# A four-network graph kernel: zeroing of the table issued behind the first loads, bit planes stored by the scalar engine with four buffers

## The reference

```python
def _L0(node_features, edge_attr, W_msg_tp, W_msg_lin, W_upd_tp, W_upd_lin, edge_index):
    row, col = edge_index
    x_j = node_features[col]
    m = einsum('ei,ej,ijh->eh', x_j, edge_attr, W_msg_tp) / sqrt(128)
    m = silu(m) @ W_msg_lin / sqrt(16)
    agg = segment_sum(m, row, num_segments=6250)
    u = silu(einsum('ni,nh,ihk->nk', node_features, agg, W_upd_tp) / sqrt(256)) @ W_upd_lin / sqrt(16)
    return node_features + u
```

## Time and profile before

| | us |
|---|---|
| median of 3 runs | 11527.22 |
| lowest, highest | 11523.59, 11538.84 |
| the profiled execution | 11525.68 |
| its span | 11523.9 |
| start, until the first matmul of the edge stage | 441.5 |
| first edge stage and N0, until the convolutions' first loads | 441.5 to 2931.4 |
| everything behind | 2931.4 to 11523.9 |

### The profile page before, as it was taken

The page is one execution under the profiler, slowest core; times in us unless marked ns, Lnnn a source line. Parts: engine busy times, 40 slices in busy tenths (PEclk is TensorE's granted clock), DMA queues, the critical chain, the costliest instruction groups (busy, mean ns, idle before and its releaser), DMA issues.

```text
span 11523.9 us, 201355 instructions
## 1 busy us (share of the span) xinstructions
PE 8973.8 (78%) x51270; PEld 6020.0 (52%) x51270; DVE 7298.7 (63%) x14361; ACT 4035.9 (35%) x11725; POOL 6700.9 (58%) x6789
## 2 busy tenths in 40 slices
PE   0499999998488998857666666688888868888886
PEld 0266666663367777742222222455555645555554
DVE  1498999995122222227777777677777767777776
ACT  2445333332000010005555555344444434444443
POOL 0588788777100000007777777577777757777775
PEclk9999999996588888855555555555555555555555
DMA  6733443440887877882222222111111111111111
GB/s 240 249 98 101 119 109 108 108 109 5 290 282 250 269 245 247 296 279 37 39 38 38 38 38 38 25 20 20 20 20 20 20 21 20 20 20 20 20 20 20
DMA packets 1340632, 1146.59 MB, mean 99 GB/s; under 512 B 329039, under 2 KB 1225504, under 8 KB 1340190
## 3 DMA queue, kind: packets, MB, share of 16 engines
q1 hardware_dynamic: 1108690, 1064.47, 29.1%
q0 software_dynamic: 210560, 44.35, 5.2%
q10 hardware_dynamic: 21186, 34.95, 1.2%
HBM read 994.01 MB, written 144.62 MB: 99 GB/s over the span
## 4 chain that ended last, share of the span: by engine, by line
POOL 31%; PE 14%; issue 12%; DMA 8%; DVE 7%; DVEq 1%; ACT 1%; SPq 1%; POOLq 0%; ACTq 0%
POOL arena L569 31%; PE ps L820 8%; DMA arena<-adj 5%; DVE msg L1779 3%; PE ps L754 2%; DVE arena L1774 2%; DMA arena<-tab,idx 2%; PE ps L935 2%; DVE acc L1266 1%; PE ps L797 1%; PE ps L633 1%; ACT x_all L1106 0%; SPq L455 0%; DMA arena<-rT 0%; DVE x_all L1606 0%
## 5 line engine op out<-in xcount | busy, mean ns | idle before, releaser
L569 POOL DMA_INDIRECT arena<-tab,idx x4896 | 4675.6, 955 | 3843.8 <-DMA idx<-in_src_p 2290.4
L935 PE MATMUL ps<-w_w2b,arena 33*128 33x256 f32 x6528 | 2928.1, 639 | 603.1 <-DMA arena<-rT 594.9
L935 PEld LDWEIGHTS ps<-w_w2b,arena 33*128 33x128 f32 x6528 | 2103.8, 330 | 1223.1 <-issue 686.9
L598 POOL DMA_INDIRECT adj<-pairs x1632 | 1868.7, 1145 | 491.4 <-issue 420.8
L1266 DVE TENSOR_TENSOR acc<-acc,ps 48x128 f32 x4920 | 1377.7, 280 | 660.0 <-DVE acc L1266 12.6
L820 PE MATMUL ps<-arena 128*128 128x192 bf16 (+1 forms) x18816 | 1341.5, 234 | 229.9 <-DMA arena<-adj 214.4
L820 PEld LDWEIGHTS ps<-arena 128*128 128x128 bf16 x18816 | 1282.7, 103 | 303.0 <-issue 293.7
L1774 DVE TENSOR_TENSOR arena<-ps,arena 128x512 f32<-128x512 f32 x1632 | 1012.8, 682 | 190.2 <-DMA arena<-tab,idx 186.6
L633 PEld LDWEIGHTS ps<-arena,threes 128*48 128x48 bf16 x4912 | 486.9, 152 | 1232.9 <-issue 1232.9
L633 PE MATMUL ps<-arena,threes 128*48 128x128 bf16 x4912 | 628.1, 309 | 642.5 <-DVE threes L1275 638.1
L1013 ACT ACTIVATE wide<-ps,not_all 128x128 bf16<-128x128 f32 x1632 | 572.8, 377 | 1241.3 <-PE ps L701 1241.1
(11 more groups left out here) (250 smaller groups left out, 10654.0 us busy)
## 6 DMA issues: line engine op xcount, KB each, us to landing
arena<-adj SPq DMA_DIRECT2D x672, 896.0 KB, 7.3
arena<-rels SPq DMA_DIRECT2D x204, 512.0 KB
arena<-tab SPq DMA_DIRECT2D x1632, 64.0 KB
adj<-zero SPq DMA_DIRECT2D x49, 2048.0 KB, 20.8
arena<-tab,idx POOLq DMA_INDIRECT x4896, 2.4
arena<-rT SPq DMA_DIRECT2D x408, 128.0 KB
adj<-pairs POOLq DMA_INDIRECT x1632
rT<-spare ACTq DMA_DIRECT2D x204, 128.0 KB
```

The lines of the kernel that those rows point to most:

```text
L569: pool.indirect_dma_start(G[b][:, u, 0:FEAT[PHASES[p]]], None, TABLE[PHASES[p]], bass.IndirectOffsetOnAxis(ap=idx[b // 2][:, b % 2 * HT + ...
L598: pool.indirect_dma_start(adj_cells, bass.IndirectOffsetOnAxis(ap=pairs[h][:, u, 0:1], axis=0), pairs16[h][:, u, 2:3], None).then_inc(cell ...
L935: last = mm(ps[:, 4 + q, (u % 2) * 256:(u % 2 + 1) * 256], row[h][0:33, u * P:(u + 1) * P], w["w2b"][:, :], start=True, stop=True)
```

## The change

SP issues 41 of the 49 zero DMAs directly behind its loads, and the last 8 (`ZEROS_LATE`) between the loads of batch 2 and batch 3 of the first edge stage. ACT now issues the stores of `rels` and the bit planes; the planes have four buffers. The columns that the 52 sums need are computed by DVE ahead of the bit planes, and ACT does the sums between its other work: ten in the bit planes, two for each chunk of A0, sixteen at the end. A0 has two buffers for its rows and two PSUM banks, is written out chunk by chunk, and PE reads the nodes directly where DVE had copied them. The helpers of the old loop, already unused, go.

```diff
+        bit16 = [x[0:T // TR, o:o + HE].bitcast(bf16) for x, o in ((arena, 2 * HE), (arena, 3 * HE), (spare, 0), (wide_flat, 0))]
+        A_ROWS = [tst[:, :, :].rearrange("p j f -> p (j f)"), stage[:, 0:CH]]
...
+        ZEROS_LATE = 8
...
-            sp.wait_ge(ready, KEYS)
-            sp.dma_start(rels, arena[0:T // TR, 4 * HE:6 * HE]).then_inc(rels_out, 16)
-            for j in range(BITS):
-                sp.wait_ge(bit_cast, j + 1)
-                sp.dma_start(bits[j, :].rearrange("(t e) -> t e", e=TR * P), bit16[j % 2]).then_inc(bits_out[j % 2], 16)
...
-            zero_table()
+            zero_table(0, NS - ZEROS_LATE)
             sp.wait_ge(w_in, 16 * LOADED)
-            sp.wait_ge(tbl_out, tables(1))
+            for j in range(2):
+                sp.wait_ge(rows_stored[j], 16 * ((NC + 1 - j) // 2))
             sp.wait_ge(rels_out, 16)
-            for j in range(2):
-                sp.wait_ge(bits_out[j], 16 * ((BITS + 1 - j) // 2))
-            edge_loads0()
+            for j, x in enumerate(bits_out):
+                sp.wait_ge(x, 16 * len(range(j, BITS, len(bits_out))))
+            edge_loads0(0, range(3))
+            zero_table(NS - ZEROS_LATE, NS)
+            edge_loads0(0, range(3, SL))
+            with sp.Fori(1, IT) as it:
+                edge_loads0(it, range(SL))
...
-            with pe.Fori(0, NC) as c:
-                step_wait(n, c, 2)
+            for c in range(NC):
+                if c >= 2:
+                    pe.wait_ge(rows_cast, c - 1)
                 for j in range(4):
-                    last = mm(ps[:, 0, j * P:(j + 1) * P], gst[0:16, j * P:(j + 1) * P], w["msg_tp"][:, :],
+                    last = mm(ps[:, c % 2, j * P:(j + 1) * P], xT[:, c * CH + j * P:c * CH + (j + 1) * P], w["msg_tp"][:, :],
                               start=True, stop=True)
...
+            def tile_signs(lo, hi):
+                for c in range(lo, hi):
+                    act_fn(signs[c % 2], first_dst, ACT.Sign, scale=-1.0, bias=n_mid[:, c:c + 1],
+                           accum_out=before_n[:, c:c + 1]).then_inc(before_in, 1)
+                    act.wait_ge(before_in, c + 1)
+
+            act.wait_ge(ready, KEYS)
+            act.dma_start(rels, arena[0:T // TR, 4 * HE:6 * HE]).then_inc(rels_out, 16)
             for j in range(BITS):
+                i, turn = j % len(bit16), j // len(bit16)
                 act.wait_ge(bit_made, j + 1)
-                if j >= 2:
-                    act.wait_ge(bits_out[j % 2], 16 * (j // 2))
-                act_fn(bit16[j % 2], bit_int[j % 2], ACT.Copy, scale=2.0, bias=-1.0).then_inc(bit_cast, 1)
+                if turn > 0:
+                    act.wait_ge(bits_out[i], 16 * turn)
+                act_fn(bit16[i], bit_int[j % 2], ACT.Copy, scale=2.0, bias=-1.0).then_inc(bit_cast, 1)
+                if j == 0:
+                    act.wait_ge(columns_in, 5)
+                if j % 2 == 1:
+                    tile_signs(j // 2, j // 2 + 1)
+                act.wait_ge(bit_cast, j + 1)
+                act.dma_start(bits[j, :].rearrange("(t e) -> t e", e=TR * P), bit16[i]).then_inc(bits_out[i], 16)
+            for c in range(NC):
+                act.wait_ge(rows_made, c + 1)
+                if c >= 2:
+                    act.wait_ge(rows_stored[c % 2], 16 * (c // 2))
+                act_fn(A_ROWS[c % 2], ps[:, c % 2, :], ACT.Copy).then_inc(rows_cast, 1)
+                tile_signs(BITS // 2 + 2 * c, BITS // 2 + 2 * c + 2)
+                act.wait_ge(rows_cast, c + 1)
+                act.dma_start(TABLE["A0"][c * CH:(c + 1) * CH, :].rearrange("(j p) f -> p j f", p=P),
+                              A_ROWS[c % 2].rearrange("p (j f) -> p j f", f=P)).then_inc(rows_stored[c % 2], 16)
+            tile_signs(BITS // 2 + 2 * NC, NH)
...
+            ts(lane[:, :], w["dummy"][:, :], float(-N), None, ALU.add).then_inc(columns_in, 1)
+            nc.vector.memset(first_dst[:, TE:], float(FAR)).then_inc(columns_in, 1)
+            nc.vector.tensor_copy(first_dst[:, 0:TE], base[:, HT:HT + TE]).then_inc(columns_in, 1)
```

More of the change, by code:

```diff
@@ L273, in build @@
         bit_cast = sem("bit_cast")
-        bits_out = [sem(f"bits_out{j}") for j in range(2)]
+        bits_out = [sem(f"bits_out{j}") for j in range(len(bit16))]
+        columns_in = sem("columns_in")
+        rows_made = sem("rows_made")
+        rows_cast = sem("rows_cast")
+        rows_stored = [sem(f"rows_stored{j}") for j in range(2)]
         adj_zeroed = sem("adj_zeroed")
@@ L363, in nodes_done @@
         def nodes_done(eng, p):
-            if PHASES[p] in WAVES:
-                for i in range(SETS):
-                    eng.wait_ge(wave_sem[i], wave_base(PHASES[p], i) + WAVES[PHASES[p]] * len(range(i, NC, SETS)))
-            else:
-                before = node[PHASES[p]]
-                eng.wait_ge(before.sem, before.at(NC - 1, before.per))
+            for i in range(SETS):
+                eng.wait_ge(wave_sem[i], wave_base(PHASES[p], i) + WAVES[PHASES[p]] * len(range(i, NC, SETS)))
+        ZEROS_LATE = 8
         CONSTS = GR * (1 + 2 + 8 + 6)
@@ L1001, in _ @@
-            before = node["A0"]
-            act.wait_ge(before.sem, before.at(NC - 1, before.per))
-            for c in range(NH):
-                act_fn(signs[c % 2], first_dst, ACT.Sign, scale=-1.0, bias=n_mid[:, c:c + 1],
-                       accum_out=before_n[:, c:c + 1]).then_inc(before_in, 1)
-                act.wait_ge(before_in, c + 1)
             act.sem_inc(scl[0].sem, SL * APER[0] - HT)
@@ L1414, in _ @@
             v = vec[0]
-            before = node[PHASES[0]]
-            dve.wait_ge(before.sem, before.at(NC - 1, before.per))
             dve.sem_inc(v.sem, (SL - 1) * VPER[0])
```

123 lines of the change are left out of this document (19 added, 104 removed).

## The result

The kernel after took 11463.98 us, median of 4 runs (11459.44 to 11470.82), against 11527.49; the ratio is 0.9947, interval 0.9935 to 0.9959. Of the rows marked * in the table of experiments, and of the kernel before beside them (14,483 and 14,698 us), every edge loop took a quarter to a third longer, so that their stage ends can't be used, their sum passes come out up to 12 us longer than elsewhere, and their ratios are to be read with care. The profiled execution has a span of 11458.2 us, 65.7 less than before.

The account below looks back on a forecast made before the run. GpSimd's scatters were taken to end the first edge stage, with DMA setting their start and the loop's end. 0.146 x 30 + 0.854 x 24 = 24.9 us off 11527.2 gave 11502 us, range 11478 to 11530.

Parts of the forecast that it names:

- E: End of GpSimd's scatters, taken to end the first edge stage near 2931 us; forecast to come 24.9 us earlier.
- dL: How much earlier the first edge stage's loop ends: 65 us from the earlier start less a 35 us stall, 30.
- ds: How much earlier GpSimd's first scatter starts in the first edge stage: forecast 24 us.
- Z': Time in the kernel after when DVE's first row load lands: forecast 375 us, range 365 to 389.
- the stall of 35 us: Edge loop's wait at batch 3, whose row load stands behind the last 8 zero blocks in SP's queue.
- s: Start of GpSimd's scatters, which need all zeros landed: forecast 436.5 us.
- b: Time that storing the bits and `rels` adds to Z': 78 us taken; 92 upper, 68 on six engines, 25 spread over all.
- Z: Time when DVE's first row load lands, behind the zeroing in SP's queue: 439.8 us in the kernel before.
- Free stores: Rival: bit stores spread over all engines or fill gaps; b 25, Z' 322, gain 78 us, 11449 us; chance 0.10.
- the starved chain: Rival: ACT's bit stores slow beside zeroing, delaying gathers and scatters; at x = 12 loss 33 us, 11560 us; chance 0.10.
- x: Time of one bit store on ACT's chain beside zeroing: 6 us taken, up to 9.2 allowed, starved from 10.
- given back: Rival: late zeros and row stores mix badly or the stall is longer; gain 0 to 11 us, 11516 to 11527; chance 0.14.

Follow-up runs that it names:

- e3: Kernel after with each of the 22 stores of `rels` and bit planes split into rows 0 to 95 and 96 to 101; 11428.94 us, ratio 0.9920.
- e12: Kernel after with all zeros issued behind the landed stores and two bit buffers in place of four; ratio 0.9997 to the kernel before.
- e1: Kernel before with 94 extra unused matmuls, moving TensorE's program by 188 instructions; 11496.96 against 11517.95 us, ratio 0.9981.
- e2: Kernel after with 34 extra unused matmuls, bringing TensorE's shift to 256 instructions against the kernel before; ratio 0.9973 to the kernel before.
- e5b: Kernel after with all 49 zero fills issued behind the landed stores, four bit buffers kept, second run; ratio 0.9960 to the kernel before.
- e10: Kernel after with all 52 ACT sums behind the table's rows, as in the kernel before; marked *, ratio 0.9972 to the kernel before.
- e10b: Kernel after with all 52 ACT sums behind the table's rows, run once more; marked *, ratio 0.9980 to the kernel before.
- e7: Kernel after with the 22 stores and the four first loads of 102 rows split into 96 and 6; ratio 0.9917 to the kernel before.
- e4: Kernel after with all 49 zero fills ahead of the first edge loads, none late; 11477.46 us, ratio 0.9961 to the kernel before.
- e6: Kernel after with two bit buffers in place of four, early zeroing kept; marked *, ratio 0.9981 to the kernel before.
- e13: Kernel after with split stores and first loads and TensorE's sum loops written out, first run; marked *, ratio 0.9936 to the kernel before.

## Why the prediction failed

- *GpSimd's scatters end the stage; E = 0.146 dL + 0.854 ds.* Right. dL = 64.9 - 35.1 = 29.8 and ds = 22.1 give 23.2, measured 28.0; from the kernel after to e3 44.6 against 42.2, from the kernel before to e12 -15.4 against -18.5. Stage ends of like kernels lie up to 5 us apart (2898.0 and 2903.3).
- *Z' = 375, the stall of 35 us, s at 436.5.* Right to within 1.2 us each.
- *The six engines and b = 78.* Right in size: splitting the stores (e3) took 45 us off Z, where b = 78 and b = 25 lie 53 apart. Free stores (322) and the starved chain (x was 5.1 us, not 10) did not come.
- *"Nothing behind 2931 is changed; I carry the shift to the end whole."* This step failed, and it carries the miss: 35.8 us of 65.7 lie behind it. No instruction is changed there, but the 188 instructions that the unrolled table rows add ahead move the sum loops, and with them the number of back branches at which TensorE stops. e1 has it alone (21 us), e2 takes it away (30 us). 33.5 of the 35.8 us lie in the three passes that lost four stops (15.7, 9.8 and 8.0). What the place is worth on the average is less: ten stops cost 2180 us of passes (two kernels), seven 2161 (six rows without *, 2156.6 to 2166.7), none 2123, and of the thirteen traces at the place of the kernel after only three had six stops, the others seven. The profiled execution was one with six, and by its 2147.1 us the quickest of them, so some luck is in the 35.8; 20 to 25 us is what the place gives in general. Whether the other three runs of the kernel after had six or seven, no trace shows.
- *The unrolled table rows "hidden".* True of their time, not of their place.
- *What earns the 25 us.* The sum came out right, with the wrong owner, and in that its fit is luck. I credited the early zeroing and held the rest to be hidden. By first scatters: ACT's issuing and sums with two buffers cost 15.4 (457.5 to 472.9), the four buffers bring 36.4 (to 436.5), the early zeroing 0.4 (436.1), the late eight 0.8 (435.3). In e12 and e5b SP also waited for landed stores, worth 2 to 3 us, so ACT's part is nearer 13 and the early zeroing's nothing. I had written that 5.3 of six engines were busy and that zeros would fill the rest; more buffers fill it as well, and once six are full the zeros need them too.
- *The 52 sums "removes nothing from a path that was limiting".* Neither shown nor refuted. I compared the gathers' end with the scatters' start only; with Z' at 375 they also meet the first loads. e10 and e10b put the first scatter 13 us later, but both are marked *, and e3 and e7 had gathers beside the first windows without a delay.
- *The rival "given back".* The late eight are nearly so: 44 us of product against a wait of 35, 3.9 us at the stage end (e4).

The Trainium skill (Runtime: NRT & Kernel Launch, Instruction fetch mechanics) says that instructions are fetched in blocks of 16 KB, in sequence, and that a taken branch whose target is no longer held forces a fetch before execution goes on. The traces agree: packets of 16 KB, 5 to 7 us without work at the loop's top, and none of it in straight code with 175 packets, though such code costs 2 to 5 us a pass. The page gives TensorE room for 2048 instructions, more than the 1698 that the trace has between two branches of this loop; between 6 and 12 of 18 branches stopped nonetheless.

## What to carry to other kernels

Read the idle time before the first instruction of every loop, and the packets of the instruction queue, before you call a stage unchanged: an edit that makes an engine's program longer or shorter moves every loop behind it. Before starting a transfer earlier, count the engines that the transfer beside it leaves free, and look whether both need the same ones; splitting 102 rows into 96 and 6 did more than all reordering. And when an experiment puts an old order back, compare its waits with those of the old kernel: here it waited for landed stores, which the old one had not.

## What the runs showed of the hardware

- A branch back to a loop of 1698 instructions on TensorE stopped it for 5 to 7 us at 6 to 12 of 18 times, by the place of the program: shifts 0 and 256 ten, 188 six or seven, 316 twelve. By the length of the passes a stop cost 7 to 9 us; the same loop written out cost 2 to 5 us a pass more than with a branch that did not stop. At 0 and 188 passes 2 and 5 had none and pass 3 three, at 316 it was the other way round; the runs don't tell why. In a pass with narrow rows the stop was followed by a second wait (6.72 and 3.00 us above).
- Stores of 102 rows held the DMA share at 0.38 of 16 engines even with four in flight (6.1 engines). The Trainium skill's rule for 102 rows (DMA: Bandwidth & Descriptors, Why a DMA increments its semaphore by 16 and not by 1) gives six, and e3's gain agrees.
- Beside GpSimd's gathers SP's issue of eight window loads took 6.03 and 6.06 us in e7 and e3, and 14 to 22 us in the four rows marked * that had both (e6, e10, e10b, e13); without gathers it took 5.52 in a row marked *.
